# Attention output kept feature-major, normalised on GpSimd batch by batch, and projected in plain float32

## The reference

```
scores = einsum('bhqd,bhkd->bhqk', Q, K) / sqrt(dk)        # 16 heads of 16 features
probs = softmax(scores, axis=-1)
intervened = probs.at[:, :, :, 0].set(0.0)
intervened = intervened / clip(intervened.sum(-1), 1e-9)
combined = probs + 0.5 * (intervened - probs)
out = einsum('bhqk,bhkd->bhqd', combined, V)
x = x + out.reshape(B, L, D) @ Wo.T + bo
```

## Time and profile before

| | |
|---|---|
| median of 3 runs | 2457.3 us (2456.31 to 2459.56) |
| profiled execution, its own time | 2459.67 us |
| its span, first to last instruction | 2457.5 us |
| TensorE matmul busy | 2135.2 us, 87% |
| VectorE / ScalarE / GpSimd busy | 71% / 55% / 27% |
| mean granted TensorE clock | 0.927 |

### The profile page before, as it was taken

How to read it: one execution, slowest core, us unless ns; L and a number is a source line. 1 busy time by engine, 2 the same in 40 slices (tenths; PEclk the granted TensorE clock), 3 DMA queues, 4 the chain that set the end, 5 groups by cost and what they waited for, 6 DMA issues and landing times. The chain is left out here.

```text
span 2457.5 us, 47833 instructions
## 1 busy us (share of the span) xinstructions
PE 2135.2 (87%) x18115; PEld 1340.6 (55%) x18115; DVE 1736.2 (71%) x2418; ACT 1346.0 (55%) x2580; POOL 651.7 (27%) x953
## 2 busy tenths in 40 slices
PE   4999599999999999689689976469999999977999
PEld 3888333333333333578578865334444444437888
DVE  7776499999999996477644479766677676617333
ACT  3443168888888888334344533226566566552444
POOL 3000513333333334400021136542232322242110
PEclk9999789999999999899899988769899999878999
DMA  4005833333342500200200013383354434011000
GB/s 130 1 0 207 201 56 58 49 49 56 43 64 39 68 13 9 73 1 0 98 12 0 0 69 137 139 117 52 57 71 69 58 56 66 14 39 41 18 26 26
DMA packets 125921, 140.42 MB, mean 57 GB/s; under 512 B 53656, under 2 KB 85272, under 8 KB 125720
## 3 DMA queue, kind: packets, MB, share of 16 engines
q1 hardware_dynamic: 117528, 129.30, 24.9%
q0 software_dynamic: 8192, 8.40, 3.1%
HBM read 81.80 MB, written 54.53 MB: 55 GB/s over the span
## 5 line engine op out<-in xcount | busy, mean ns | idle before, releaser
L1290 DVE TENSOR_REDUCE att_maxes<-att_s_max 128x2 f32<-128x1024 f32 (+2 forms) x832 | 968.7, 1179 | 223.3 <-PE att_s_max L1140 120.9
L1270 ACT ACTIVATE att_probs<-att_s_exp 128x512 f32<-128x512 f32 (+3 forms) x1792 | 886.5, 550 | 335.3 <-PE att_s_exp L1180 167.8
L1204 PE MATMUL att_o_ps<-att_probs,att_v_st 128*32 128x256 f32 (+1 forms) x6912 | 538.9, 384 | 53.2 <-DVE att_o_n L1320 44.2
L1180 PE MATMUL att_s_exp<-att_q_st,att_k_st 64*128 64x512 f32 (+3 forms) x1792 | 467.8, 484 | 5.6 <-ACT att_probs L1270 3.3
L1140 PE MATMUL att_s_max<-att_k_st,att_q_st 62*128 62x512 f32 (+3 forms) x1792 | 403.9, 426 | 71.2 <-DMA att_k_st<-k_parts 57.8
L1180 PEld LDWEIGHTS att_s_exp<-att_q_st,att_k_st 64*128 64x128 f32 x1792 | 193.4, 188 | 356.8 <-ACT att_probs L1270 279.2
L1204 PEld LDWEIGHTS att_o_ps<-att_probs,att_v_st 128*32 128x32 f32 x6912 | 139.4, 109 | 301.0 <-issue 130.9
L1140 PEld LDWEIGHTS att_s_max<-att_k_st,att_q_st 62*128 62x128 f32 x1792 | 194.7, 200 | 93.0 <-issue 60.3
L1451 POOL DMA_DIRECT2D attention_rows<-att_o_out x256 | 166.5, 657 | 59.4 <-issue 40.8
L583 DVE TENSOR_TENSOR ffn1b_h_lo<-ffn1b_h,ffn1b_h_hi 128x512 fp32r<-128x512 f32 x64 | 44.5, 696 | 112.2 <-PE ffn1b_acc L134 100.3
L583 DVE TENSOR_TENSOR ffn1a_h_lo<-ffn1a_h,ffn1a_h_hi 128x512 fp32r<-128x512 f32 x64 | 45.0, 705 | 99.5 <-PE ffn1a_acc L134 76.3
(11 more groups left out here) (308 smaller groups left out, 4299.7 us busy)
## 6 DMA issues: line engine op xcount, KB each, us to landing
att_q_st<-q_parts SPq DMA_DIRECT2D x384, 64.0 KB, 5.6
att_k_st<-k_parts SPq DMA_DIRECT2D x192, 128.0 KB, 5.1
q_parts<-qkv_parts SPq DMA_DIRECT2D x32, 512.0 KB, 3.4
k_parts<-qkv_parts SPq DMA_DIRECT2D x32, 512.0 KB, 2.7
v_rows<-qkv_vt SPq DMA_DIRECT2D x16, 512.0 KB, 2.8
att_v_raw<-v_rows SPq DMA_DIRECT2D x32, 256.0 KB, 6.5
attention_rows<-att_o_out POOLq DMA_DIRECT2D x256, 32.0 KB, 2.5
x<-in_x SPq DMA_DIRECT2D x8, 512.0 KB, 9.0
```

The source lines that it names most:

```text
L1180: mm = pe.matmul(s_exp[:, plan.bank[place], q0:512], k_st[rows, it.set, pr, kt * P:(kt + 1) * P], q_st[rows, it.set, qc, pr, q0:512], star ...
L1204: mm = pe.matmul(o_ps[j * VW:(j + 1) * VW, cols], v_st[:, it.par, kt, j, :], probs[:, step % 2, j, cols], start=kt == 0 and part == 0, sto ...
L1270: act.activation(probs[:, step % 2, j, q0:512], s_exp[:, plan.bank[place], q0:512], ACT.Exp, scale=1.0 if causal else 0.25).then_inc(s["ex ...
L1290: v.tensor_reduce(maxes[:, qc, :, pairs, qt - 4 * qc, kc], banks, AX.X, ALU.max).then_inc(s["max_done"], 1)
```

## The change

- ScalarE copies `o_ps` whole into one of two SBUF tiles (`copy_out`), at the places where VectorE turned it. VectorE's turns and reciprocals of each qc go. GpSimd stores the copy in one DMA of 256 KB, features and sums as rows.
- When a batch is complete, GpSimd fetches it during the next batch's iterations: the sums as 128 x 128 tiles, the features into `o_t`, which holds all tokens feature-major. The weights are worked out on the compact tiles (two reciprocals on VectorE a batch in att0, one in att1), stored to DRAM, read back repeated over the 16 features of each head (`spread_weights`: a DMA for each kind of weight and half of the features, 256 KB each), and GpSimd multiplies (`normalise_outputs`). The last batch's part of this lies in the out stage.
- The out stage multiplies `o_t` with Wo directly in plain float32: 64 matmuls of 256 columns a stage, without load, turn or split. The add of bo moves into the first batch's iterations of attention. Wo is no longer split at load.
- SETS is 3, and `stage` runs two iterations ahead. GpSimd splits the maxima of qc = 1 ahead of `put_values`. SyncE no longer waits for the stores at the end of attention; the first rows of the values are loaded by four GpSimd DMAs at its start.

The two reciprocals of the last batch stand behind the adds and statistics of chunks 1 and 2. The diff, cut:

```diff
-SETS = 4
+SETS = 3
...
+def fetch_outputs(p, E, b, last):
+
+    n = E.o_sem
+    p.wait_ge(n["stored0"], 16 * (GROUPS * (b + 1) + (0 if last else 1)))
+    p.wait_ge(n["stored1"], 16 * GROUPS * (b + 1))
+    rows = E.o_dram[b].rearrange("g (j r) s -> (g j) r s", r=VW)
+    for kind in range(E.kinds):
+        p.dma_start(E.sums[:, kind, :], rows[:, HD + kind, :].rearrange("h (c t) -> h c t", t=P)).then_inc(n["sums_in"], 16)
+    for k in range(KD):
+        p.dma_start(E.o_t[:, k, b * S:(b + 1) * S], rows[k * H // KD:(k + 1) * H // KD, 0:HD, :]).then_inc(n["o_in"], 16)
...
+def invert_totals(v, E, b):
+    n = E.o_sem
+    if E.kinds == 1:
+        v.wait_ge(n["sums_in"], 16 * (b + 1))
+        if b:
+            v.wait_ge(n["weights_out"], 16 * b)
+        v.reciprocal(E.weights[:, 0, :], E.sums[:, 0, :]).then_inc(n["weights"], 1)
+        return
+    v.wait_ge(n["total"], b + 1)
+    v.reciprocal(E.total_inv[:, :], E.total[:, :]).then_inc(n["total_inv"], 1)
...
+def shares(p, E, b):
+    n = E.o_sem
+    p.wait_ge(n["total_inv"], b + 1)
+    p.tensor_tensor(E.share[:, :], E.sums[:, 0, :], E.total_inv[:, :], ALU.mult).then_inc(n["step"], 1)
+    p.wait_ge(n["step"], 4 * b + 1)
+    p.tensor_scalar(E.share[:, :], E.share[:, :], CLIP, None, ALU.max).then_inc(n["share"], 1)
+    p.tensor_scalar(E.w_all[:, :], E.total_inv[:, :], 1.0 - LAMBDA, None, ALU.mult).then_inc(n["step"], 1)
+    p.wait_ge(n["step"], 4 * b + 2)
+    if b:
+        p.wait_ge(n["weights_out"], 16 * b)
+    p.tensor_tensor(E.weights[:, 1, :], E.w_all[:, :], E.sums[:, 1, :], ALU.mult).then_inc(n["step"], 1)
...
+def store_weights(p, E, b):
+    n = E.o_sem
+    if E.kinds == 2:
+        p.wait_ge(n["share_inv"], b + 1)
+        p.wait_ge(n["step"], 4 * b + 3)
+        p.tensor_tensor(E.w_add[:, :], E.share_inv[:, :], E.w_all[:, :], ALU.mult).then_inc(n["step"], 1)
+        p.wait_ge(n["step"], 4 * b + 4)
+        p.tensor_tensor(E.weights[:, 0, :], E.w_add[:, :], E.w_all[:, :], ALU.add).then_inc(n["weights"], 1)
+    p.wait_ge(n["weights"], b + 1)
+    p.dma_start(E.w_dram[b, 0:E.kinds].rearrange("n h (c t) -> (h c) n t", t=P), E.weights[:, :, :]).then_inc(n["weights_out"], 16)
...
+def normalise_outputs(p, E, b, half):
+    n, c = E.o_sem, 2 * b + half
+    PER = 4
+    rest = E.o_t[:, :, c * CHUNK:(c + 1) * CHUNK]
+    p.wait_ge(n["wide_in"], 16 * KD * E.kinds * (c + 1))
+    p.wait_ge(n["o_in"], 16 * KD * (b + 1))
+    if E.kinds == 1:
+        p.tensor_tensor(rest, rest, E.wide[:, 0, :, :], ALU.mult).then_inc(n["normal"], 1)
+        p.wait_ge(n["normal"], c + 1)
+        return
+    if c == 0:
+        p.wait_ge(n["first_in"], 16 * B)
+    p.tensor_tensor(rest, rest, E.wide[:, 0, :, :], ALU.mult).then_inc(n["product"], 1)
+    p.wait_ge(n["product"], 3 * c + 1)
+    for k in range(KD):
+        p.tensor_scalar(E.wide[:, 1, k, :], E.wide[:, 1, k, :], E.v_first[:, b, k:k + 1], None, ALU.mult).then_inc(n["product"], 1)
+        p.wait_ge(n["product"], 3 * c + 2 + k)
+    p.tensor_tensor(rest, rest, E.wide[:, 1, :, :], ALU.add).then_inc(n["normal"], 1)
+    p.wait_ge(n["normal"], c + 1)
...
-                    if left >= 3:
-                        if not first:
-                            sp.wait_ge(s["st_ready"], plan.pieces(it, 0, 0))
-                        stage(it.ahead(3))
+                    if left >= 2 and not first:
+                        sp.wait_ge(s["st_ready"], plan.pieces(it, 0, 0))
+                        stage(it.ahead(2))
...
-                sp.wait_ge(s["o_stored"], 2 * 16 * GH * ITERS)
...
-                            pe.wait_ge(s["o_turned"], it.n(2, qc))
+                            pe.wait_ge(s["o_copied"], it.n(2, qc))
...
+                def copy_out(it, qc):
+
+                    act.wait_ge(s["pv_done"], it.n(NS, plan.begin[qc + 1]))
+                    if it.r:
+                        act.wait_ge(o_stored[qc], 16 * it.r)
+                    act.activation(o_sb[:, qc, :], o_ps[:, :], ACT.Copy).then_inc(s["o_copied"], 1)
...
+                        if step == 1 and not first:
+                            copy_out(it.ahead(-1), 1)
+                        if step == plan.begin[1] + 1:
+                            copy_out(it, 0)
...
-                def turn_out(it, qc, first=False):
-
-                    v.wait_ge(s["pv_done"], it.n(NS, plan.begin[qc + 1]))
-                    if not (first and qc == 0):
-                        v.wait_ge(s["o_done"], it.n(2, qc))
-                    v.transpose(o_n[:, :, :].rearrange("p b r -> p (b r)"), o_ps[:, :]).then_inc(s["o_turned"], 1)
...
-                        if step == 1 and not first:
-                            turn_out(it.ahead(-1), 1)
-                        if step == plan.begin[1] + 1:
-                            turn_out(it, 0, first)
+                        if it.r >= GROUPS and step == 6 and it.hg == 1:
+                            invert_totals(v, E, it.b - 1)
+                        if it.r >= GROUPS and step == 2 and it.hg == 2 and not causal:
+                            invert_shares(v, E, it.b - 1)
...
-                    p.wait_ge(s["o_done"], it.n(2, qc + 1))
-                    for j in range(GH):
-                        head = (it.hg * GH + j) * HD
-                        rows = E.ao_dram[bass.ds(it.b * S + qc * 512, 512), head:head + HD]
-                        p.dma_start(rows.rearrange("(t r) d -> r t d", r=32),
-                                      o_out[32 * j:32 * j + 32, :, :]).then_inc(s["o_stored"], 16)
+                    p.wait_ge(s["o_copied"], it.n(2, qc + 1))
+                    p.dma_start(E.o_dram[it.b, it.hg, :, qc * 512:(qc + 1) * 512], o_sb[:, qc, :]).then_inc(o_stored[qc], 16)
...
                 def body(it, first, last):
+                    b = it.b - 1
+                    split_max(it, 1)
+                    if not first:
+                        store(it.ahead(-1), 1)
                     if not last:
                         put_values(it.ahead(1), not first)
-                    if first:
-                        split_max(it, 1)
-                    if not first:
-                        normalise_out(it.ahead(-1), 1, True, (it, 1))
-                        store(it.ahead(-1), 1)
-                    normalise_out(it, 0, not first, None if last else (it.ahead(1), 0))
+                    if b < 0:
+                        add_bias(2 * it.hg)
+                    elif it.hg == 1 and not causal:
+                        total_sums(p, E, b)
+                    elif it.hg == 2:
+                        store_weights(p, E, b)
+                    elif it.hg == 3:
+                        normalise_outputs(p, E, b, 0)
+                        spread_weights(p, E, b, 1)
                     store(it, 0)
-
+                    if not last:
+                        split_max(it.ahead(1), 0)
+                    if b < 0:
+                        add_bias(2 * it.hg + 1)
+                    elif it.hg == 0:
+                        fetch_outputs(p, E, b, False)
+                    elif it.hg == 1 and not causal:
+                        shares(p, E, b)
+                    elif it.hg == 2:
+                        spread_weights(p, E, b, 0)
+                    elif it.hg == 3:
+                        normalise_outputs(p, E, b, 1)
...
+            for c in range(CHUNKS):
+                pe.wait_ge(E.o_sem["normal"], c + 1)
+                if c >= 2:
+                    pe.wait_ge(s["x_new"], 2 * (c - 1))
                 for t in range(CT):
                     for k in range(KD):
-                        mm = three_pass(pe, acc[:, par, t, :], pair(E.xt, slice(None), par, k, slice(t * P, (t + 1) * P)),
-                                        pair(E.wo, slice(None), k, slice(None)), k == 0, k == KD - 1)
+                        at = (c * CT + t) * P
+                        mm = pe.matmul(acc[:, c % 2, t, :], E.o_t[:, k, at:at + P], E.wo[:, k, :], start=k == 0, stop=k == KD - 1)
                 mm.then_inc(s["out_done"], 1)
-
-            def body(c, par, use, fresh):
-                turn_rows(c, par, use, fresh and par == 0)
-                if not (fresh and par == 0):
-                    product(c - 1, 1 - par, fresh)
-
-            each_chunk_of_two(pe, body)
-            product(CHUNKS - 1, 1, False)
-            turn(pe, E, T, CHUNKS, 0, s, ready=1)
+                if c == TURN_AT:
+                    turn(pe, E, T, 0, 0, s, True)
...
+                if c == 1:
+                    invert_totals(v, E, LAST)
+                    norm_rstd(v, E, s["next_step"], s["next_std"], NEXT, n)
+                if c == 2:
+                    if E.kinds == 2:
+                        invert_shares(v, E, LAST)
+                    normalise(v, E, 0, 0, s)
+                if c == TURN_AT:
+                    part_lo(v, E, T, 0, 0, s)
...
+            fetch_outputs(p, E, LAST, True)
+            if E.kinds == 2:
+                total_sums(p, E, LAST)
+                shares(p, E, LAST)
```

(4 more changed lines are left out.)

217 lines of the change are left out of this document (73 added, 144 removed).

## The result

The changed kernel takes 2377.3 us (median of 4, 2374.46 to 2378.16) against 2458.4 us of the kernel before: ratio 0.9663, 95% interval [0.9642, 0.9684]. The forecast was 2357, the range 2332 to 2402. The profiled execution spans 2375.1 us, 82.4 less than before.

A forecast was written before the change was run, and what follows sets the result against it. TensorE, 87% busy, bounds the kernel, in att0 with ScalarE, neither having slack. Gains 15.8 + 23 + 28 + 24.7 + 7 + 2 = 100.5 take the profiled 2459.67 to 2359.2, median 2357 us; range 2332 to 2402.

The forecast's parts named there:

- a slow clock: Rival for att1: the clock stays low because its falls have another cause, 28 us less gained, 2385 us; chance 0.18.
- dear products: Rival in out stages: float32 weight loads not hidden, product 0.48 + 2 x 0.19 us, 2393; chance 0.13 including dearer chain.
- Att0: First attention: value products wait less for the bank, stall 0.87 to about 0.36 us, 31 times, 15.8 us gained.
- Att1, waits and clock: Second attention: of 28.3 us of waits about 5 remain, 23 gained; falls of the granted clock vanish, 28 more.
- GpSimd and VectorE hidden in attention: In attention, GpSimd's batch work and VectorE's added reciprocals hide behind other work; cost nothing.
- Staging: Loads into three buffers in att1: there after 21 us, first needed after 26.4 or 23; no cost.
- that rival: Staging in att1 becomes a wait: loads take 29 us instead of 21, kernel slower at 2490 us; chance 0.04.
- Price of plain float32: Out stages: one product of 256 columns costs 0.48 us, a chunk of eight 3.84 us.
- a dearer chain of GpSimd and DMAs: Out stages: other half of the rival at 2393 us, GpSimd's chain dearer; chance 0.13 shared with dearer float32.
- Out1: After the second attention: 39.3 us from last value product to next stage, a gain of 24.7.
- Out0: After the first attention: 57.5 us from last value product to next feed-forward, a gain of 7.
- The start of ffn1b gets 2 us of clock back: Start of ffn1b: with TensorE busy shortly before, perhaps 2 us of clock regained.

The follow-up runs named there:

- e5: The changed kernel with the whole copy of the attention output made by VectorE, where the turn stood, instead of ScalarE; 2444.5 us.
- e6: The changed kernel with the copy of the attention output made three times in att1, each waiting for the one before, att0 untouched; 2460.7 us.
- e1: The changed kernel with VectorE's reciprocal of the last batch's sums ahead of its first out-stage chunk and that of the shares behind that chunk; 2363.4 us.
- e4: The changed kernel with a second wide tile in the out stage, so GpSimd issues both halves' spreads before normalising the first; 2366.1 us.
- e2: The changed kernel with the very last store of each attention issued by SyncE instead of GpSimd; 2372.1 us.

## Why the prediction was right or wrong

The time is within the range, 20 us above the forecast. The mechanisms of attention hold with their sizes, and two terms of the out stages account for the miss. It is more than the forecast's own spread of 15 us; it lies in the range because that was drawn wide enough for two other cases, a slow clock and dear products, which did not occur.

- **Att0: right.** Iterations of 41.2 us, as forecast, instead of 42.2; waits of 8.9 us in 31 (0.29 each) instead of 24.2. It gives 14.9 us, where 15.8 were forecast. e5 shows the reason.
- **Att1, waits and clock: right.** 23 + 28 = 51 were forecast, 53.9 came. Waits 5.3 us in 16, where 5 were said. In sizes: an iteration without falls went from 33.03 to 31.27, 16 x 1.76 = 28 us, 5 more than the 23 forecast for the waits. The other 26 of the 53.9 are what the falls cost, some 28, less the 2 us of reciprocals below. The rival of the clock fell: with the 1.38 us stall gone no iteration has a fall, and with stalls put back (e5, e6) they return. The Trainium skill ("TensorE: Matmul & The Clock Gate", HAM oscillation) states its rule for idle gaps longer than any stall inside att1; runs of this kernel show falls with stalls of 1.35 to 1.56 us, so the measurement decides.
- **GpSimd and VectorE hidden in attention: no wait on GpSimd shows, but VectorE is 2.5 us off.** The three iterations of att1 that hold its one reciprocal, 0.94 us, take 31.98 instead of 31.3, and the three of att0 that hold the reciprocal of the shares 41.35 instead of 41.21: 2.5 us together, counted at nothing. No run takes the reciprocals away.
- **Staging: right.** TensorE has no wait on loads inside att1, so that rival falls.
- **Price of plain float32: right.** A chunk takes 3.69 us at full clock, for 3.84. Weight loads hide, and the half of the rival that has dearer products falls; its other half, a dearer chain of GpSimd and DMAs, is what out0 shows.
- **Out1: too small a chain.** 39.3 forecast, 47.0 measured. The first step, "TensorE runs chunks from 2.5", came at 6.8: what closes the stage was not priced. The reciprocal, to be done at 14.0, was done 20.4 us after the last value product, behind two chunks on VectorE. First half normal 24.8, measured 30.3; second 32.4, measured 38.2. Chunk 7 took 5.4 us at a granted clock of 0.68, where 3.8 had been counted.
- **Out0: the term that failed, also in sign.** 57.5 forecast, a gain of 7; 71.7 measured, a loss of 6.4. By its own steps, from the last value product: reciprocal done at 14.0, measured 21.4; weights stored at 21.9, seen by GpSimd at 30.0; first half normal 35.2, measured 46.4; second 48.5, measured 62.3. So 7.4 us stand in front of the end of the reciprocal: 5.8 are the closing of the stage, the rest mostly the first chunk, which TensorE runs at a granted clock of 0.69. The steps up to the stored weights make 0.7. The last 5.7 are two spreads of 8.3 and 7.5 us instead of 6.5 and two normalisations of 8.1 instead of 6.8 (a 128x512 product with a scalar takes 1.61 us, not 1.06). Chunk 7 took 5.6 us for the 6 counted. e1 and e4 take 7.0 and 6.0 us off out0, and the two together with e2 20.2, so it is this chain that sets the length of out0.
- **The start of ffn1b gets 2 us of clock back: wrong.** From its first matmul to the end it is 0.6 us shorter than before.

Against the terms of the sum out0 is 13.4 us worse, out1 7.4, ffn1b 1.4, att0 0.9; att1 is 2.9 better, starts and other feed-forwards 2.1. That makes 18.1: 100.5 forecast, 82.4 measured in the span. The rest of the 20 us lies between the profiled executions and the medians. No run takes back the plain float32 product of the out stages or the third buffer alone, so what each of these is worth rests on the traces.

## What to carry to other kernels

When an engine releases a buffer on which the bottleneck waits, ask what stands ahead of that release in the engine's queue, not how long the operation takes: the same copy cost 67 us more on VectorE. Where a stage boundary exposes a chain over several engines and DMAs, walk it instruction by instruction in each engine's own order, and price the closing of the stage: two reciprocals moved ahead of work that could wait were worth 14 us, 12.5 of them seen in the two out stages. A stall that is short against an iteration can cost as much again through the clock (here some 28 us and 28), so look at the granted clock by iteration, not only over the span.
